# Selective-scan stages of a fused four-layer kernel: where the weighting of x by dt is done, which engine takes the low parts of the weights, and a new order inside the scan's rounds

## The reference, cut to what matters

```python
proj = hidden_states @ in_proj_w
gate, hbc, dt = ...                       # 4096, 4096 + 2*128, 64 columns
hbc = silu(conv4(hbc) + conv_b)           # causal, 4 taps
x, Bm, Cm = ...                           # x: 64 heads x 64
dt = softplus(dt + dt_bias);  A = -exp(A_log);  dA = dt * A
cum = cumsum(dA) within a chunk
decay  = exp(cum_i - cum_j)  for i >= j
scores = (C_i . B_j) * decay * dt_j
Y_diag = scores @ x
states = sum_l exp(cum_last - cum_l) * dt_l * B_l x_l
Y = Y_diag + exp(cum) * (C . state before) + D * x
out = (rmsnorm(Y * silu(gate)) * norm_w) @ out_proj_w
```

## Time and profile before

| what | value |
|---|---|
| median of three runs | 1966.46 us |
| profiled execution | span 1943.9 us; the page gives no other time for it |
| median less span | 22.6 us |
| busy share PE / DVE / ACT / POOL | 87% / 75% / 63% / 46% |
| `ssd3`, steady part | from about 1240 to 1750 us, a group of two jobs each 69.2 us |
| mean granted TensorE clock | 0.926; 1.00 in the steady part of `ssd3` |

### The profile page before, as it was taken

The page is one execution under the profiler, slowest core; times in us unless marked ns, Lnnn a source line. Parts: engine busy times, 40 slices in busy tenths (PEclk is TensorE's granted clock), DMA queues, the critical chain, the costliest instruction groups (busy, mean ns, idle before and its releaser), DMA issues. The chain is left out here.

```text
span 1943.9 us, 29621 instructions
## 1 busy us (share of the span) xinstructions
PE 1691.9 (87%) x10866; PEld 1350.1 (69%) x10866; DVE 1457.5 (75%) x3045; ACT 1222.1 (63%) x2463; POOL 891.9 (46%) x870
## 2 busy tenths in 40 slices
PE   6899579979994667798878998899999999997899
PEld 4799257858992356696667886667777777775788
DVE  7888687577886766686677667678788888877576
ACT  4587247646871269317932544888988989887443
POOL 0775541107856300301722220267788787878321
PEclk9999789989996779798989998999999999999799
DMA  8797214117973100000020100000100000000111
GB/s 306 230 294 241 66 55 150 51 35 235 295 228 92 60 1 2 1 1 0 1 97 1 37 30 1 23 12 22 34 17 23 28 23 20 25 14 1 45 49 36
DMA packets 74605, 139.86 MB, mean 72 GB/s; under 512 B 11476, under 2 KB 52564, under 8 KB 73428
## 3 DMA queue, kind: packets, MB, share of 16 engines
q1 hardware_dynamic: 63700, 108.50, 16.9%
q0 software_dynamic: 10752, 29.37, 5.3%
HBM read 113.72 MB, written 24.12 MB: 71 GB/s over the span
## 5 line engine op out<-in xcount | busy, mean ns | idle before, releaser
L79 PE MATMUL ps<-H_r,wt_r 128*128 128x512 f32 (+1 forms) x732 | 284.6, 429 | 11.7 <-ACT wt L87 4.7
L79 PE MATMUL ps<-work_r 128*128 128x256 f32 (+2 forms) x1200 | 248.0, 297 | 6.7 <-DVE work_r L91 2.6
L87 ACT ACTIVATE work<-ps 128x512 f32<-128x512 f32 (+3 forms) x354 | 168.1, 498 | 120.4 <-PE ps L79 103.3
L91 DVE TENSOR_TENSOR work<-work,ps 128x512 f32<-128x512 f32 (+4 forms) x304 | 170.7, 562 | 90.9 <-ACT work L87 57.6
L79 PE MATMUL ps<-wt,work 128*128 128x256 f32 (+1 forms) x1120 | 221.0, 372 | 20.4 <-POOL work L91 10.0
L99 DVE SCALAR_TENSOR_TENSOR wt<-ps,wt 128x511 f32<-128x511 f32 (+2 forms) x234 | 174.3, 747 | 47.2 <-ACT wt L87 41.1
L79 PEld LDWEIGHTS ps<-work_r 128*128 128x128 f32 (+1 forms) x1200 | 189.8, 187 | 28.6 <-DVE work_r L91 11.4
L79 PEld LDWEIGHTS ps<-wt,work 128*128 128x128 f32 (+1 forms) x1120 | 168.4, 201 | 44.6 <-ACT work L87 10.0
L79 PEld LDWEIGHTS ps<-H_r,wt_r 128*128 128x128 f32 (+1 forms) x732 | 139.8, 191 | 63.0 <-issue 14.5
L91 POOL TENSOR_TENSOR work<-work 128x256 f32<-128x256 f32 (+2 forms) x160 | 131.8, 827 | 108.1 <-ACT work L87 87.6
L87 ACT ACT_TABLE_LOAD x113 | 145.0, 1283 | 47.7 <-DVE lmv L119 29.2
(11 more groups left out here) (255 smaller groups left out, 4203.0 us busy)
## 6 DMA issues: line engine op xcount, KB each, us to landing
ering<-in_moe_w SPq DMA_DIRECT2D x87, 624.0 KB, 5.8
ye<-work SPq DMA_DIRECT2D x64, 256.0 KB, 4.6
wt<-in_ssd_wg SPq DMA_DIRECT2D x64, 128.0 KB, 2.2
ye<-early SPq DMA_DIRECT2D x1, 4096.0 KB, 14.6
wt<-in_ssd_wg SPq DMA_DIRECT2D x8, 512.0 KB, 3.6
Hd<-H SPq DMA_DIRECT2D x16, 128.0 KB, 1.7
wt<-in_ret_fc SPq DMA_DIRECT2D x2, 1024.0 KB, 11.7
work<-Hd,work POOLq DMA_INDIRECT x128, 4.8
```

What stands on the lines that cost most here:

```text
L79: self.last = self.e.matmul(o, l, r, start=start, stop=stop, skip_group_check=True)
L87: self.last = self.e.activation(o, a, f, **kw)
L91: self.last = self.e.tensor_tensor(o, a, b, op)
```

## The change

1. ScalarE's copy of the transposed x out of PSUM (`xt`) goes away. In its place VectorE multiplies x straight from the bank by dt into `xq`, which now has five buffers (it had two; the five buffers of the copy, `q.xt`, go).
2. GpSimd's multiplication by dt goes away. It now makes only `xw`, from `xq`; `wd` therefore no longer holds dt, and one VectorE instruction ahead of the rounds goes, with its wait.
3. The low parts of the next group's weights (`split`) go from VectorE to GpSimd, except for the first group. `conv` and `z` on TensorE wait for GpSimd there.
4. The layout of dA (`scan0`) is a step of its own at the end of the round ahead of `scan`.
5. The table `ROUND` has another order: `y`, `square`, `E`, `merge`, `decay`, `mask` follow each other, behind `S`, `add` and `state`, and ahead of `conv` and `z`.

```diff
-            q.xc, q.sz, q.xt = some(q.nx, 4, 512), some(q.nx, 4, 512), some(5, 512)
+            q.xc, q.sz, q.xq = some(q.nx, 4, 512), some(q.nx, 4, 512), some(5, 512)
...
-        ROUND = (("add", 3), ("wo", 3), ("E", 0), ("gate", 2), ("state", 1), ("x", 0), ("scan", -5), ("keep", 0), ("S", 1), ("xt0", -2), ("decay", 0), ("merge", 1), ("conv", -7), ("silu", -3), ("split", -8), ("scale", -1), ("sum", 2), ("square", 2), ("y", 1), ("z", -7), ("mask", 0), ("xd", 0), ("xt", -3))
+        ROUND = (("wo", 3), ("gate", 2), ("x", 0), ("scan", -5), ("keep", 0), ("S", 1), ("xt0", -2), ("add", 3), ("state", 1), ("y", 1), ("square", 2), ("E", 0), ("merge", 1), ("decay", 0), ("mask", 0), ("conv", -7), ("silu", -3), ("split", -8), ("scale", -1), ("sum", 2), ("z", -7), ("xd", 0), ("xt", -3), ("scan0", -6))
...
-                pe.wait_ge(V, "split", si, g, c4)
+                pe.wait_ge(G if g else V, "split", si, g, c4)
...
-                pe.wait_ge(G, "xq", si, n)
+                pe.wait_ge(V, "xq", si, n)
...
-                a.act(q.xt[n % 5], b.ap, ACT.Copy).then_inc(A, "xt", si, n).frees(b)
...
-            elif step == "scan":
+            elif step == "scan0":
                 four = q.dA[:, 4 * b_:4 * b_ + 4, g * 8:g * 8 + 8]
...
+            elif step == "scan":
                 b, sc = ps.of("cumT", si, j), wts["scan_c"]
...
+        def low_xz(e, si, q, g, c4):
+            w, h = [x.rearrange("p c (u n) -> p c u n", u=2)[:, :, :, cols(c4)] for x in (q.xz, q.hi2)]
+            e.wait_ge(A, "split", si, g, c4)
+            for c in range(2):
+                e.tt(rnd(w[:, c, :, :]), w[:, c, :, :], f32(h[:, c, :, :]), ALU.subtract).then_inc(e.done, "split", si, g, c4)
...
+            elif step == "xt":
+                b = ps.of("xt", si, n)
+                if n >= 5:
+                    v.wait_ge(PE, "y", si, n - 5)
+                    v.wait_ge(G, "xw", si, n - 5)
+                v.wait_ge(PE, "xt", si, n)
+                v.tt(v8(q.xq[n % 5]), v8(b.ap), bc(q.dt[:, t, g * 8:g * 8 + 8].unsqueeze(2), [128, 8, 64]), ALU.mult)
+                v.then_inc(V, "xq", si, n).frees(b)
...
-                g_.tt(v8(q.xq[n % 2]), x, bc(q.dt[:, t, heads].unsqueeze(2), [128, 8, 64]), ALU.mult).then_inc(G, "xq", si, n)
...
-                    g_.tt(v8(q.xw[m % 2]), x, bc(q.wd[:, t, heads].unsqueeze(2), [128, 8, 64]), ALU.mult)
+                    g_.tt(v8(q.xw[m % 2]), v8(q.xq[n % 5]), bc(q.wd[:, t, heads].unsqueeze(2), [128, 8, 64]), ALU.mult)
```

More of the change, by code:

```diff
@@ L2358, in ssd_buffers @@
             q.R2, q.L = some(2, 4, 128), some(2, 2, 128)
-            q.st, q.xq, q.xw, q.sq = (some(2, 512) for _ in range(4))
+            q.st, q.xw, q.sq = (some(2, 512) for _ in range(3))
             q.y = some(3, 512)
@@ L2399, in ssd_order @@
                         continue
-                    if step in ("silu", "xd", "scan", "scale") and n % 4:
+                    if step in ("silu", "xd", "scan0", "scan", "scale") and n % 4:
                         continue
@@ L2547, in pe_unit @@
                 pe.wait_ge(V, "W", si, n)
-                pe.wait_ge(G, "xq", si, n)
+                pe.wait_ge(V, "xq", si, n)
                 for h in range(8):
                     strip = slice(64 * (h % 2), 64 * (h % 2) + 64)
-                    pe.mm(b[strip, cols(h // 2)], q.xq[n % 2][:, h * 64:(h + 1) * 64], q.E[n % 2][:, h, :], True, True)
+                    pe.mm(b[strip, cols(h // 2)], q.xq[n % 5][:, h * 64:(h + 1) * 64], q.E[n % 2][:, h, :], True, True)
                 pe.then_inc(PE, "y", si, n)
@@ L2663, in v_unit @@
                 v.tt(E, E, bc(q.STm[:, b_, c4, :].unsqueeze(1), [128, 8, 128]), ALU.mult).then_inc(V, "W", si, n)
[L2664 to L2668, removed]
+            elif step == "split" and g == 0:
+                low_xz(v, si, q, g, c4)
+            elif step == "xt":
[6 more added lines that the diff above has]
+                v.then_inc(V, "xq", si, n).frees(b)
             elif step == "conv":
@@ L2731, in g_unit @@
             heads = slice(g * 8, g * 8 + 8)
[L2732 to L2736, removed]
-                g_.tt(v8(q.xq[n % 2]), x, bc(q.dt[:, t, heads].unsqueeze(2), [128, 8, 64]), ALU.mult).then_inc(G, "xq", si, n)
+            if step == "split" and g:
+                low_xz(g_, si, q, g, c4)
+            elif step == "x":
                 if c4 < 3:
                     m = state_of(j, c4)
+                    g_.wait_ge(V, "xq", si, n)
                     if m >= 2:
                         g_.wait_ge(PE, "S", si, unit_of(m - 2))
-                    g_.tt(v8(q.xw[m % 2]), x, bc(q.wd[:, t, heads].unsqueeze(2), [128, 8, 64]), ALU.mult)
+                    g_.tt(v8(q.xw[m % 2]), v8(q.xq[n % 5]), bc(q.wd[:, t, heads].unsqueeze(2), [128, 8, 64]), ALU.mult)
                     g_.then_inc(G)
@@ L2782, in ready @@
             e.wait_ge(A, "wd", si)
-            e.wait_ge(V, "wd", si)
         def pe_ssd(pe, si):
```

2 lines of the change are left out of this document (removed).

## The result

The changed kernel takes 2009.22 us (median of 4 runs, 2007.04 to 2012.9), the kernel before 1965.99 us (4 runs, 1961.54 to 1967.33): ratio 1.0223, 95% interval 1.021 to 1.0237, so 2.2% slower.

What follows compares the result with a forecast made beforehand. TensorE was taken as the bound, ScalarE second. Seven groups with `split` gave +39 us, the eighth -1, the ends -4, `ssd2` -1, together +33: 2000 us from 1966.5, range 1957 to 2024.

Steps and rivals of the forecast that it cites:

- the lag: Late start of `decay` in round 1 of a job with `split`, carried over from round 0: 0.7 us.
- the ring: In `split` jobs `square` waits for GpSimd's low parts, `sum` and `gate`; TensorE waits 6.7 us in all; chance 0.64.
- the terms: Group with `split`: TensorE's work 65.6, small gaps 0.9, waits 6.7 and 0.85, together 74.05 us; with the clock 5.6 longer.
- The clock: TensorE's clock falls to 1.2 GHz around the running sum's wait: 0 to 1.6 us each, 0.8 taken.
- rival 5: TensorE's clock stays down longer: 3 us more a group, 2020 us; chance 0.07.
- the eighth group: The one group without `split`: 68.2 us, -1 against the kernel before.
- The ends: Rounds without `conv` and `z`, where GpSimd loses a multiplication of 1.0 to 1.3 us: -4 us, 0 to -8.
- The strips: TensorE goes in and out of strips once a round, not twice: 0.15 us saved a round, 1.2 a group.
- The relief of ScalarE: ScalarE, 4 x 0.5 us a job lighter, decides and the kernel gets faster: 1940 us; chance 0.14.
- rival 2: Lighter ScalarE decides: TensorE's waits shrink from 2.5 to 0.9 us a group, 1940 us in all; chance 0.14.
- VectorE as the bound through `mask`: `mask` ahead of the taps of `conv` holds VectorE: 0.5 us a round more, up to 2030 us; chance 0.10.
- Ring and relief: The two cancel: a wait of 2 us per `split` job instead of 6.7, 1964 to 1969 us; chance 0.05.

Runs made afterwards that it cites:

- e2: Changed kernel with the low parts of the weights back on VectorE, all else kept: 1941.7 us against 1947.03 for the kernel before.
- e1: Changed kernel with `split` (high and low parts) ahead of `silu` in the table: 1954.24 us against 1947.03 for the kernel before.
- e8: Changed kernel with `sum` ahead of `split` in the table: 1980.52 us against 1966.98 for the kernel before.
- e3: Changed kernel with `square` back behind `sum` in the table, low parts still on GpSimd: 1946.6 us against 1947.03 for the kernel before.
- e11: Changed kernel with the table order `sum`, `split`, `silu`, low parts still on GpSimd: 1939.72 us against 1947.05 for the kernel before.
- e6: Changed kernel with the old table order, dA laid out inside `scan` and low parts on VectorE: 1958.26 us against 1966.98 for the kernel before.
- e5: Kernel before with only the new table order, without `scan0`: 1989.05 us against 1966.98 for the kernel before.
- e4: Changed kernel with the layout of dA (`scan0`) ahead of `square`: 1974.46 us against 1947.03 for the kernel before.
- e10: Changed kernel with low parts on VectorE, dA laid out three rounds earlier, `z` ahead of `split`: 1968.24 us against 1969.64 for the kernel before.

## Why the prediction was right, and where its sizes were off

The mechanism is shown: taking away any one link gives back most of the loss. Of 42.5 us of stage, 47.0 go without the low parts on GpSimd (e2), 36.3 without silu ahead of them (e1), 29.2 without `sum` behind them (e8), 38.0 with `square` out of the wait (e3). In numbers, with zero at round 1's strips (1424.92):

| step | predicted | measured |
|---|---|---|
| `decay` of round 1 starts (0.5 and the lag) | 1.2 | 2.0 |
| high parts done | 10.2 | 10.9 |
| low parts done | 11.4 | 12.9 |
| `sum` done | 13.2 | 14.6 |
| `gate` done | 14.5 | 15.9 |
| `decay` of round 2 starts | 15.0 | 16.5 |
| running sum's matmul | 21.1 | 22.6 |
| ScalarE idle ahead of `square` | 3 to 4 | 4.51 |
| TensorE waits ahead of the running sum | about 4.7 | 4.41 |
| ScalarE's busy time a group | -4.5 | -4.0 |
| a group with `split` | 73 to 76 | 76.0 to 77.3 |

**The low parts** were taken at 0.6 us each from the row of another GpSimd instruction. Here they are the term that was mis-sized: 1.86 us for the pair in this place, 793 ns as the mean over four groups. Undisturbed, one takes 0.72 to 0.74 (all 48 in e11 between 1300 and 1750 us); of this pair the first takes 0.73 and the second 1.17. The row of the view by lines (busy us, mean ns of one, idle time before it):

```profile
L91 POOL TENSOR_TENSOR wt_r<-wt,wt_r 128x256 fp32r<-128x256 f32 x33 | 25.5, 793 | 59.6 <-ACT wt_r L87 59.6
```

The second runs while VectorE has an instruction that reads two SBUF tiles, a 128x512 `work<-work,wt` of 0.76 at 1436.44. The same form in round 0 takes 1.42 and in e11 1.41. **The lag** was worked out from the same 1.2 and came to 0.7, and is 1.5; with the longer pair ScalarE stands 1.61 us for GpSimd at the `square` of round 1 already, a wait that I had costed only by difference of round lengths.

**A wait was overlooked**: the transposes at 1433.58 belong to the next job's first unit and need silu. They start 2.51 us behind `S`, some 1.65 to 2.1 of it waiting, the largest wait of TensorE before the running sum. It didn't move the sum of a job with `split`, since TensorE meets the ring at the running sum anyway: by the terms such a period is (65.6 + 0.9) / 2 + 6.7 = 39.95, measured 40.85. In the other jobs it is about 0.4.

**The clock** was taken at 0.8 a group. The rows show one fall to 1.2 GHz in each group with `split`, at the end of the running sum's wait or within 1 us behind it. At 0.5 the eight matmuls of `off` take 1.71 us from start to start (1448.05 to 1449.76) against 0.89 (1430.18 to 1431.07), and `S` 1.27 against about 0.95: with the running sum itself some 1.5 us. In two of six groups the clock stays down for 6.8 us (1522.1 to 1528.9, 1675.7 to 1682.5), and just the periods behind those are 36.32 and 36.43, where the others are 35.1 to 35.4. So a longer fall costs 1.1 us more; that is rival 5 in small. Before has no fall in its steady groups. The period without `split` is 35.65 on the mean, against 34.1 + 0.8 by the terms.

**The count.** Six groups are longer by 42.8 us together, 7.1 each and not 5.6; the seventh job with `split`, in the run-up, costs 1.4 and not 5.6. Two errors of opposite sign: 7 x 5.6 = 39 against 44.2. Two other periods of the run-up are shorter, by 1.9 together (-1 taken for the eighth group). **The ends** were given -4, and were -0.2 ahead of the first running sum and -2.5 from the last to the next stage's projection (97.1 us before, 94.6 after). The stall of the earlier trace rows was not the longest there. That one stands ahead of the last `wo` but one, whose `gate` comes behind a low part of 2.82 us that GpSimd makes for the next stage. After, this low part holds up only the last `wo`, and for less (before, then after):

```profile
1798.75 3.78 PE L79 MATMUL ps<-wt,work 128*128 128x256 f32 x8 [5.79 <-POOL work L91]
```

```profile
1866.16 3.78 PE L79 MATMUL ps<-wt,work 128*128 128x256 f32 x8 [2.13 <-POOL work L91]
```

At the place of the earlier trace rows, where TensorE stood 3.23 us for GpSimd, it now stands 2.07 us for silu:

```profile
1814.24 0.66 PE L83 MATMUL ps<-cst,wt 128*128 128x128 f32 x4 [2.07 <-ACT wt L87]
```

This is the wait that was overlooked in the steady groups. Later it stands 2.05 and 1.90 us ahead of `y`, for VectorE, where before had 1.28 at most. `ssd2` was +1.2 (up to the start of `ssd3`) instead of -1; why is open. In all: the groups +5.0, the ends +1.4, `ssd2` +2.2 and the eighth group -0.9 over the terms are 7.7 us. With the sum's 33 (its parts add up to 33, and 33.5 only rounds to 2000) that is the 41.0 us which the two profiles show behind `ssd2`'s first running sum; 43.2 lie between the medians. That the time came out 9 us from the forecast is in part luck, as the job of the run-up (1.4 for 5.6) hid a part of what the six groups cost more.

**The strips** were right: `y` takes 1.02 from start to start as before, the strips 0.43, and a round saves about 0.2 us (0.15 taken, 0 to 0.22 as bounds), for the entrance behind `wo` is gone (1.73 in place of 1.82) and the first matmul of z is followed after 0.23 and not 0.34. The passage from `y` to the exponents costs 0.10: the last of the 16 starts 0.20 before the strips, where the pairs ahead of it follow each other at 0.10. Before the whole array it was 0.20 as well. The Trainium skill (TensorEngine Tiling (Array Packing), Tiling Modes) says that changing the mode drains TensorE; the trace agrees for a change from column strips to row strips, with these 0.10 us. The saving was near the upper bound all the same, and not near the lower one as the prediction had it by that rule.

**The rivals.** The relief of ScalarE doesn't decide in the kernel after. e6 has it alone and is ahead of before (0.9957), though not in its steady groups, where VectorE takes over as the one waited for. With the ring open e2 and e11 give 0.9969 and 0.9963; there the groups are shorter too (68.4 and 68.5 us). The three are not told from each other by their intervals. That is a quarter to a third of what rival 2 would have it (1940 from 1966, 0.9865). VectorE as the bound through `mask` isn't in the trace of after; it is in e5, where ScalarE's copies and VectorE's low parts are both still there. Ring and relief don't cancel in after; e3, at 1.0003, comes to zero without the ring, by other waits: in each group TensorE stands 1.23 us ahead of the third exponent matmul for ScalarE's copy of z, and 0.63 in the other job.

What stays open is where half of e6's 0.43% comes from, why a group of e8 is 1.6 us shorter than the least forecast, and how much of the 1.3 us a group by which e2 is ahead of e6 comes from the strips (0.2 us a round would be 1.6 a group) and how much from waits.

## What to carry to other kernels

Where engines run lists in a fixed order, moving work to an idle engine adds a link to whatever that engine's queue already feeds; write down the queue of the receiving engine between the moved instruction and the next one that anybody waits for, and add it up. A 4 us wait costs nothing or everything by its place: put the long instruction (silu) between the producer of the moved work's input and the consumer of what stands behind it, so that it covers the round trip. And test a table of steps with its neighbours: three entries in another order were worth 49.6 us of 644.2, and turned 2.2% slower into 0.4% faster.

## What the runs showed of the hardware that I had not expected

Elementwise instructions on GpSimd and VectorE stretch each other. VectorE's 128x1024 `mask` takes 1.22 us at its shortest, and about 2.0 in 12 of its 51 rows of e5 between 1300 and 1750 us. At 1452.30 it is 2.02, beside these on GpSimd:

```profile
1452.19 1.04 POOL L91 TENSOR_TENSOR ering_r<-wt,work_r 128x512 fp32r<-128x512 f32 x1
1453.19 2.26 POOL L91 TENSOR_TENSOR work<-work 128x256 f32<-128x256 f32 x2
```

The second is 1.26 where it isn't disturbed. The low parts on VectorE take 1.02 for two at 1446.66, where GpSimd falls idle during them, and 2.21 for two at 1456.46, where it is busy throughout. The Trainium skill (GPSIMD Engine Reference, Key points) says that GpSimd shares its SBUF interfaces with VectorE, with contention where a VectorE instruction has two SBUF inputs; `mask` and the low parts have two such inputs, and the rows agree and give the size, up to a factor of 2 on either side. No run here measured it by itself.

The kernel before takes 1947.0 us (17 runs each) on two chips, and 1967.0 and 1969.6 (8 and 23 runs) on two others, 1% apart, five times the difference that a comparison on one chip can tell. The profiles show where: the first running sum of `ssd2`, ahead of which these kernels hardly differ, stands at 895 to 902 us in e1 to e4 and e11, and at 918 to 923 in e5 to e10 and after. Why is open.
